# A graph layer's last stage rearranged: where the chain's steps stand, one more portion of final rows, eight PSUM banks in turn

## What is computed

```python
h = jnp.maximum(_layernorm(x, axis=-1), 0.0)
x_i = h[dst]; x_j = h[src]
msg = jnp.concatenate([x_i, x_j - x_i], axis=-1) @ W.T + b
x = x + segment_max(msg, dst)
```

## Time and profile before

| what | us |
|---|---|
| median of 3 runs | 879.14 |
| the profiled execution | 878.57 |
| its span, first to last instruction | 876.9 |
| lists, first part of the chain, trees (start of the span to the first round) | 302.5 |
| dense stage, tiles 0 to 18, with trees | 248.1 |
| dense stage, tiles 19 to 48 | 292.8 |
| behind the last round | 33.6 |

### The profile page before, as it was taken

The page is one execution under the profiler, slowest core; times in us unless marked ns, Lnnn a source line. Parts: engine busy times, 40 slices in busy tenths (PEclk is TensorE's granted clock), DMA queues, the critical chain, the costliest instruction groups (busy, mean ns, idle before and its releaser), DMA issues.

```text
span 876.9 us, 8002 instructions
## 1 busy us (share of the span) xinstructions
PE 547.9 (62%) x2442; PEld 264.7 (30%) x2442; DVE 801.8 (91%) x1290; ACT 408.1 (47%) x244; POOL 619.9 (71%) x631
## 2 busy tenths in 40 slices
PE   2564896000000468777777767788888888888852
PEld 1553565000000123322233323333333333333331
DVE  7989999999999799998899899999999998888985
ACT  3786213000039055775675769755555756351000
POOL 2677277887777767777777777777777677777742
PEclk9999999555555599998899888999999999999985
DMA  8951003323364665665554556555656654453655
GB/s 261 204 150 25 8 21 94 90 59 92 86 194 97 182 194 174 175 171 137 174 157 149 171 138 175 173 179 170 185 172 193 217 193 150 148 176 79 95 108 166
DMA packets 114694, 126.75 MB, mean 145 GB/s; under 512 B 19542, under 2 KB 96836, under 8 KB 114379
## 3 DMA queue, kind: packets, MB, share of 16 engines
q1 hardware_dynamic: 95090, 86.33, 32.3%
q0 software_dynamic: 19376, 38.94, 18.6%
q10 hardware_dynamic: 184, 0.96, 0.3%
HBM read 86.43 MB, written 40.57 MB: 145 GB/s over the span
## 4 chain that ended last, share of the span: by engine, by line
DVE 33%; PE 17%; issue 13%; DMA 1%; ACT 1%; POOL 0%; DVEq 0%; POOLq 0%; SPq 0%
DVE acc L1291 19%; PE ps L852 17%; DVE maxima L1235 10%; DVE hT L1244 2%; DVE hT L1258 1%; DMA ohs<-winners 1%; ACT ohs L598 1%; DVE hT L1249 1%; DVE hT L1349 1%; DMA hT<-running_max,end_row 0%; DMA running_max<-maxima 0%; POOL hT L705 0%; POOLq L197 0%; DVEq L1290 0%; DVE hT L1351 0%
## 5 line engine op out<-in xcount | busy, mean ns | idle before, releaser
L726 POOL DMA_INDIRECT rows<-near_table,idx x503 | 516.5, 1027 | 181.2 <-issue 134.6
L1291 DVE TENSOR_TENSOR acc<-ps,acc 128x1924 f32<-128x1924 f32 x196 | 344.1, 1780 | 34.7 <-PE ps L852 34.4
L852 PE MATMUL ps<-ohs,near 128*128 128x481 fp8e3 x1404 | 319.3, 381 | 77.4 <-DVE acc L1291 68.9
L598 ACT ACTIVATE ohs<-ohs,spike 128x6272 fp8e3<-128x6272 uint8 x36 | 197.8, 5513 | 82.3 <-DMA ohs<-winners 82.3
L852 PEld LDWEIGHTS ps<-ohs,near 128*128 128x128 bf16 x1404 | 134.2, 100 | 262.5 <-DVE acc L1291 88.9
L1235 DVE SCALAR_TENSOR_TENSOR maxima<-maxima,fresh,rows 128x128 f32<-128x128 f32 x503 | 176.4, 351 | 13.7
L593 ACT ACTIVATE hT<-k,off 128x1600 bf16<-128x1600 int16 (+6 forms) x49 | 65.9, 1392 | 205.8 <-DVE hT L1249 182.8
L852 PE MATMUL ps<-sorts_mem,near 128*128 128x481 fp8e3 x507 | 117.7, 387 | 28.6 <-DVE acc L1291 26.7
L840 PE MATMUL ps<-flags,ones 128*128 128x10 f32 x2 | 0.6, 360 | 150.3 <-DVE spare L1269 150.3
L598 ACT ACTIVATE sorts_mem<-sorts_mem,spike 128x6272 fp8e3<-128x6272 uint8 x13 | 71.7, 5515 | 23.2 <-DMA sorts_mem<-winners 23.2
L852 PEld LDWEIGHTS ps<-sorts_mem,near 128*128 128x128 bf16 x507 | 49.4, 102 | 96.6 <-DVE acc L1291 31.1
(11 more groups left out here) (182 smaller groups left out, 461.7 us busy)
## 6 DMA issues: line engine op xcount, KB each, us to landing
running_max<-maxima SPq DMA_DIRECT2D x63, 512.0 KB, 3.7
ohs<-winners SPq DMA_DIRECT2D x36, 784.0 KB, 6.5
sorts_mem<-winners SPq DMA_DIRECT2D x13, 784.0 KB, 6.5
rows<-near_table,idx POOLq DMA_INDIRECT x503, 3.2
acc<-in_x SPq DMA_DIRECT2D x6, 512.0 KB, 7.2
near_table<-acc SPq DMA_DIRECT2D x12, 256.0 KB, 4.5
base<-in_x SPq DMA_DIRECT2D x1, 2744.0 KB
out_x<-hT SPq DMA_DIRECT2D x12, 224.0 KB
```

The lines of the kernel that those rows point to most:

```text
L598: nc.scalar.activation(oh[t % OHS], oh_bytes[t % OHS], ACT.Abs_reciprocal_sqrt, bias=spike[:, 0:1], scale=float(SPIKE), saturate=False).th ...
L726: nc.gpsimd.indirect_dma_start(rows[:, n % (SLOTS * GATHERS), :], None, near_table[:, :], bass.IndirectOffsetOnAxis(idx[:, n:n + 1], 0)).t ...
L852: last = nc.tensor.matmul(bank(4 * (n % 2) + c - UNITS[r][0])[:, 0:CHUNK], near[:, t, part, :], oh[t % OHS][:, at:at + CHUNK], start=part ...
L1291: V.tensor_tensor(into, found[:, 0:z - a, 0:CHUNK], into, ALU.max).then_inc(max_done, 1)
```

## The change

Three constants of the planner, one more cut, and the banks of the last transposes. The price of a gather in the planner goes from 1.3 to 1.26 us behind rounds and from 1.4 to 1.3 behind trees. `CUTS` gets the entry (47, 496): columns 44 to 46 need only steps below 496, and one more flag checks it, so `flags` has 11 columns. Transposes and joins use eight banks in turn, and group g of the transposes waits for join g-8.

```diff
-CUTS = ((36, 400), (44, 472), (49, 504))
+CUTS = ((36, 400), (44, 472), (47, 496), (49, 504))
...
-            pieces += [("round", (2.15, 1.65, 1.65, 1.65)[r], 1.3)]
+            pieces += [("round", (2.15, 1.65, 1.65, 1.65)[r], 1.26)]
         if trees < 25:
-            pieces += [(name, cost, 1.4) for name, cost in tree_pieces(trees)]
+            pieces += [(name, cost, 1.3) for name, cost in tree_pieces(trees)]
...
-        flags = sb("flags", [P, 10], F32)
-        flag_s = sb("flag_s", [P, 10], F32)
+        flags = sb("flags", [P, 11], F32)
+        flag_s = sb("flag_s", [P, 11], F32)
...
-            def finals(g):
-                a, z = spans[g]
+            def finals(a, z):
                 cap = next(cap for cut, cap in CUTS if z <= cut)
                 for j in range(a, z):
                     nc.gpsimd.indirect_dma_start(
                         rowsF[:, j, :], None, running_max[0:cap * P, :],
-                        bass.IndirectOffsetOnAxis(end_row[:, j:j + 1], 0)).then_inc(final_in[g], 16)
+                        bass.IndirectOffsetOnAxis(end_row[:, j:j + 1], 0)).then_inc(final_in[j // GROUP], 16)
...
-            stored(CUTS[1][1] // STEPS)
-            for g in range(early_groups, waiting_groups):
-                finals(g)
-            stored(all_blocks)
-            for g in range(waiting_groups, groups):
-                finals(g)
+            for (a, _), (z, cap) in zip(CUTS, CUTS[1:]):
+                stored(cap // STEPS)
+                finals(a, z)
...
-                if g >= 4:
-                    pe.wait_ge(joined, g - 3)
+                if g >= 8:
+                    pe.wait_ge(joined, g - 7)
                 for j in range(a, z):
-                    last = nc.tensor.transpose(bank(g % 4)[:, (j - a) * D:(j - a + 1) * D],
+                    last = nc.tensor.transpose(bank(g % 8)[:, (j - a) * D:(j - a + 1) * D],
                                                acc[:, j:j + (P - 1) * tiles + 1:tiles], ident[:, :])
...
                 if h:
-                    for c, (cut, most_steps) in enumerate(CUTS[:2]):
+                    for c, (cut, most_steps) in enumerate(CUTS[:-1]):
                         then(V.tensor_scalar(flags[:, 6 + c:7 + c], tot[:, cut - a:cut - a + 1], float(most_steps - first - 1), None,
                                              ALU.is_gt))
-                    for at_cut, (cut, most_steps) in zip((a, CUTS[0][0], CUTS[1][0]), CUTS):
+                    for at_cut, (cut, most_steps) in zip([a] + [cut for cut, _ in CUTS], CUTS):
                         then(V.tensor_scalar(end_f[:, at_cut:cut], tot[:, at_cut - a + 1:cut - a + 1], float(first),
                                              float(most_steps - 1), ALU.add, ALU.min))
```

More of the change, by code:

```diff
@@ L171, in edgeconv @@
     CT = sum(c for _, _, c in PARTS)
-    early_groups, waiting_groups = (cut // GROUP for cut, _ in CUTS[:2])
+    early_groups = CUTS[0][0] // GROUP
     spans = [(a, min(a + GROUP, tiles)) for a in range(0, tiles, GROUP)]
@@ L309, in edgeconv @@
         count_ps = bank(7)[:, 256:257]
-        flag_ps = bank(7)[:, 0:10]
+        flag_ps = bank(7)[:, 0:11]
         x_pad_set = sem("x_pad_set")
@@ L733, in _ @@
                         stored(CUTS[0][1] // STEPS)
-                    finals(g)
+                    finals(*spans[g])
                 if (b + 1) * GATHERS == decide_at:
@@ L1066, in loser_flags @@
                 then(V.scalar_tensor_tensor(std[:, a:z], S1[:, 0, a:z], 0.0, twice_mean[:, a:z], ALU.is_ge, ALU.mult,
-                                            accum_out=flags[:, 8 + h:9 + h]))
+                                            accum_out=flags[:, 9 + h:10 + h]))
                 then(V.tensor_scalar(J, S, 7, None, ALU.logical_shift_right))
@@ L1347, in join @@
                 dve.wait_ge(final_in[g], 16 * (z - a))
-                found = bank(g % 4)[:, 0:(z - a) * D].rearrange("p (j d) -> p j d", d=D)
+                found = bank(g % 8)[:, 0:(z - a) * D].rearrange("p (j d) -> p j d", d=D)
                 V.tensor_tensor(rowsF[:, a:z, :], found, rowsF[:, a:z, :], ALU.max).then_inc(joined, 1)
```

## The result

| | before | after |
|---|---|---|
| median us (runs) | 879.14 (7) | 873.03 (7) |
| lowest to highest | 876.09 to 880.07 | 872.39 to 875.21 |
| span of the profiled execution | 876.9 | 871.0 |
| first round starts at | 302.5 | 301.9 |
| tiles 0 to 18 | 248.1 | 252.4 |

The ratio is 0.9941, with an interval from 0.9924 to 0.9957: 0.6% faster. 873.4 was forecast.

The account below looks back on a forecast made before the run. VectorE's work plus its waits was taken as the bound. Terms -9.1 + 4.3 - 1.5 + 0.7 + 0.3 = -5.3 gave span 871.6; with 1.67 us outside the span, 873.4 us was forecast, range 869 to 880.

Parts of the forecast that it names:

- The end, -9.1 forecast: Behind the last round: 7 steps, 13 joins in a row and the last store take 24.5 us instead of 33.6.
- 5.2 us of storing and completion follow: After the last join: 5.2 us until the span's end, kept unchanged in the sum for the new end.
- Worth nothing: Extra portion of final rows in the end: no gain once the steps are moved, costed at 0, between 0 and -0.5.
- Tiles 0 to 18, +2.8 forecast: Twelve steps moved here as three blocks cost VectorE +4.3 us, with -1.5 for parts falling into waits for TensorE.
- rival A: Tiles 0 to 18: longer TensorE gaps beside trees lower its clock, giving back 4 to 6 us: 878; chance 0.20.
- Tiles 19 to 48, +0.7 forecast: Same step counts in reordered tiles: 189.6 us before, 190.3 after, so +0.7, between -2 and +2.
- the prices of the forms: Tile time by which rounds steps follow: "0404" 9.62 us, "4040" 10.19, "4004" 10.2, "4400" about 11.1.
- rival C: Chain steps wait for late gathers, half the blocks of tiles 19 to 34 by 1 us or so: +15, 888; chance 0.08.
- Flags, +0.3 forecast: VectorE's list work: one more flag and one more piece of `end_f`, two instructions of about 0.14 us, unhidden.
- Rival B: The end is bound by stores at 249 GB/s; a rate 10 to 15% lower adds +2 to +3: 876; chance 0.12.
- D: More hidden: new blocks all fall into waits (-2.8), "4400" costs no more than "4040" (-1.8): 868.8; chance 0.14.
- E: In the end, the portion of final rows and the eight banks have no effect of their own; changes no number.

Follow-up runs that it names:

- place_only: The kernel before with only the planner's prices changed (1.26 and 1.3), old cuts, four banks: 873.54 us, ratio 0.9930.
- warm_fillers: The changed kernel plus nine unread matmuls per tile in tiles 1 to 19, behind the second round, into an unused bank: 866.14 us, ratio 0.9852.
- odd_rounds: The changed kernel with chain steps only behind the second and fourth round of a tile from tile 19 on: 867.07 us, ratio 0.9853.
- after_again: The changed kernel, unchanged, measured a second time: 873.62 us, ratio 0.9930 to the kernel before.
- banks_only: The kernel before with only eight banks in turn for the transposes behind the last round: 879.83 us, ratio 1.000.

## Why the prediction was right, and where not

*The end, -9.1 forecast, -11.4 measured.* The mechanism was right: 7 steps, 13 joins at 1.33 us, no wait for final rows. The step that failed is "5.2 us of storing and completion follow" the last join: a term of the sum that was 2.1 us too large. I took the 5.2 us for the price of a store. Their end was set by GpSimd: before, its last final row ends at 868.14,

```profile
867.20 0.94 POOL L705 DMA_INDIRECT hT<-running_max,end_row  x1 [0.30 <-issue]
```

and 8.8 us later is 876.9, the end of the span. After, GpSimd is done at 857.61, which would give 866.4, and the stores set the end, 3.1 us behind the last join. That is 2.1 of the 2.3 us by which the forecast gain of the end was too small. Before the change, then, the last join was not what the end waited for, and the 4.9 us of VectorE's wait were not all on the path to the end. For the same reason the portion's margin was overstated: I had the final rows 3.0 us ahead of the joins, but that counted only to the joins. In `place_only` GpSimd's end gives 862.87 + 8.8 = 871.7 against a span of 872.4, so 0.7 us were left. "Worth nothing" held, by less than I said.

*Tiles 0 to 18, +2.8 forecast, +4.3 measured.* The three blocks cost 3.7 us of VectorE's busy time, of the 4.3 priced, and its idle time grew by 0.6. The -1.5 for waits that they would fall into didn't come: 14.8 us of waits for TensorE, 3.2 of them at the first round, against 15.2 and 4.1 before. `warm_fillers` shows what these waits hang on: with the clock held up 8.1 us of them go, so it is the clock more than the form. The mean clock of the stage is 0.89 against 0.90; in the trace's clock records the lower level lasts for 54.6 us of the stage, against 48.3 before. That the new blocks beside trees lengthened TensorE's idle stretches and so cancelled what the forms gave (rival A, at most 1.5 us instead of the 4 to 6 it was sized at) fits this, but no run separates it.

*Tiles 19 to 48, +0.7 forecast, +1.8 measured.* `odd_rounds` bears out the prices of the forms. Two things were missing: tile 19, right behind a tree, takes 10.8 us, not the 9.62 of its form: most of its first matmuls run at the lower clock, which lasts from 556.7 to 560.2; and in tiles 24 and 25 1.0 us went, most of it to a late gather, which `after_again` does not have (rival C, small). The row:

```profile
612.47 1.51 DVE L1231 SCALAR_TENSOR_TENSOR maxima<-maxima,fresh,rows 128x128 f32<-128x128 f32 x4 [0.67 <-DMA rows<-near_table,idx]
```

*Flags, +0.3 forecast:* the first round starts 0.6 us earlier, at 301.86 against 302.46; over all fourteen profiles it lies between 301.9 and 303.8, so the term can't be told from the spread.

*Rival B*, the stores as a bound, did not happen: SyncE's last store follows the last join by 1.5 us. *D* would have needed what `warm_fillers` and `odd_rounds` do on purpose. *E* is true of the banks and, beside the moved steps, of the portion. So the mechanism of the forecast held, but that 873.4 was met at 873.0 is luck: two errors cancel, the end 2.3 us too pessimistic and the dense stage 2.6 too optimistic, beside 0.9 of start and flags.

The Trainium skill ("TensorE: Matmul & The Clock Gate", "HAM oscillation") names idle gaps of TensorE as the cause of a low clock, and as the cure a loop order, or a larger matrix, that keeps TensorE busy. The runs here agree on the cause: with the gaps filled the mean clock of tiles 0 to 18 goes from 0.89 to 0.98, and the time falls by 7.5 us. What it says on cycling through banks in the loop of the matmuls is not tested here: `banks_only` (1.000) changes the last transposes alone, and both of its kernels turn through banks.

## To carry to other kernels

Look at what each engine's last instruction is before reading a tail: an engine that finishes late can set the end although nobody waits for its last instruction, as GpSimd did here with its 8.8 us, and moving its last work forward can then be worth more than the wait that the profile shows. Two measures against one wait don't add up; test them alone and together. When one engine alternates between feeding another and its own work, where its own work stands in the cycle can be worth as much as how much of it there is, and cheap filler work on the idle partner can pay by keeping its clock.

## What the runs showed of the hardware

- In none of the fourteen profiles does the span end before 8.8 us have passed after the last instruction of GpSimd (8.8 in six of them and behind a memset of 0.1 us, more where something else was later). Behind SyncE's last store it ends after 1.5 to 2.0 us where GpSimd is done early enough.
- 171 matmuls that nobody reads, 37.8 us of TensorE's busy time, made the kernel 7.5 us faster (873.62 to 866.14). The mean granted clock of tiles 0 to 18 went from 0.89 to 0.98.
- GpSimd's queue of indirect DMAs, which waits for its landings and for VectorE, reached step 320 at 564.4 and at 560.7 us in two runs of the same kernel.
